# Two expert layers: rows taken and put by tables over the slots, in place of scatters and gathers over the tokens

## Chip, core and metric

One core of a Trainium2 chip runs the whole kernel. The metric is the device time of one execution in microseconds (us), the median of several. Engines: TensorE (PE in the profile; PEld is its weight load), VectorE (DVE), ScalarE (ACT), GpSimd (POOL) and the queue of SyncE (SPq). All DMAs of the core are moved by the same 16 DMA engines.

## What is computed

Twelve residual sublayers, each followed by a layer norm, over x of 2 x 1024 tokens by 256 features. The change touches two of them, both mixtures of 8 experts with a hidden size of 1024:

```python
def _L1_ffn_ref(x, wr, br, w1, b1, w2, b2):        # each token goes to one expert
    expert_id = argmax(x @ wr + br)
    y[e] = gelu(x @ w1[e] + b1[e]) @ w2[e] + b2[e]
    return y[expert_id]
def _L2_ffn_ref(x, Wr, W1, W2):                    # each token has two, of 640 places each
    probs = softmax(x @ Wr); topk_probs, topk_experts = top_k(probs, 2)
    for e in range(8):
        g, idx = top_k(gates of the tokens that chose e, 640)
        y = y.at[idx].add(g * (relu(x[idx] @ W1[e]) @ W2[e]))
    return y
```

## The kernel before

`x_tok` (128 x 16 x 256, f32) holds x by token in SBUF: tile n has tokens 128n to 128n + 127. Each expert layer has two stages with a barrier between them, a router stage and an experts stage.

**Router stages** (`top1_router_stage`, from L1717; `top2_router_stage`, from L1821). VectorE works through a chain of small steps, each waiting for the one before (`step`), with a few products by TensorE between. The result is `core.slots`: for each token, and for each of its choices, the row (slot) that it has in a buffer sorted by expert, plus `slot_gates`. In the first layer also `group_rows`, the expert whose weights each group of slots needs. SP loads the next stage's early data (`following.load`, L1745) meanwhile.

**Experts stages** (`sparse_experts_stage`, L1476). A group is a run of slots of one expert. The first layer (`choices == 1`, `dynamic`) has 15 groups: 7 times a pair of 128-slot tiles and then a single tile, and a last pair. The second (`choices == 2`) has 8 groups of 5 tiles. Every group needs one load of weights of 2180 KB, in one of two buffers `w`.

1. POOL sends each of the 16 tiles of `x_tok` (twice in the second layer) by an indirect DMA to its slots in the DRAM buffer `slot_tokens` (`core.xg`), L1674. In the first layer it first issues the weights of groups 0 and 1 (`weights`, L1666).
2. When all have landed (semaphore `scattered`), SP loads the slots of groups 0 and 1 (L1529). In the second layer SP also issues the weights (L1534).
3. For each group, TensorE transposes its tiles (`turn`, L1560; VectorE copies them out, L1623), multiplies by w1 (`up`, L1573; ScalarE's activation, L1610) and by w2 (`down`, L1585; VectorE adds b2, L1632). The order is up(g), turn(g+1), down(g). When group g is done, SP stores it to `slot_outputs` (`core.yg`, L1543), and then come the weights (POOL in the first layer, L1666, SP in the second) and the slots (SP) of group g+2.
4. When the last store has landed, POOL gathers the outputs of each token tile by `slots` into `got`, a ring of 8 (L1687), VectorE adds each to `x_tok` with its gate (`mix`, L1644 and L1648), and the tail does the layer norm: statistics by VectorE (L2718, L2722), roots by POOL (L2728, L2730, put among the gathers by `ROOTS`), norm by VectorE (L2738), transposes by TensorE (L2749), copies by ScalarE (L2756).

`clear_slots` (L128) zeroes 5120 KB and 4096 KB of the two DRAM buffers during an early attention stage.

Of the kernel before, what the change touches and what calls it, by code (L numbers as in the profile page):

```python
# [24 lines left out]
P = 128  # L25
B, T, D = 2, 1024, 256
N = B * T
# [51 lines left out]
class Core:  # L79


    def __init__(self, nc, A):
# [508 lines left out]
def head_mixing_stage(nc, core, early, room):  # L591
# [10 lines left out]
    with Mem(nc, "L0_attn") as m:  # L602
# [38 lines left out]
        def _(sp):  # L641
# [14 lines left out]
            sp.dma_start(core.spare[:], A["spare"]).then_inc(core.loaded, 16)  # L656
            sp.wait_ge(core.loaded, 32)
# [203 lines left out]
def masked_heads_stage(nc, core, early, bit):  # L861
# [11 lines left out]
    with Mem(nc, name) as m:  # L873
# [27 lines left out]
        @block.sync  # L901
        def _(sp):
            bit.load(sp)
            clear_slots(core, sp)
# [571 lines left out]
def sparse_experts_stage(nc, core, name, func, choices, order, dynamic, keys):  # L1476
# [19 lines left out]
    RING = 8  # L1496
    with Mem(nc, name) as m:
# [9 lines left out]
        got = m.sb("got", [P, RING, choices, D])  # L1507
# [7 lines left out]
        ROOTS = {11: (0,), 15: (1, 2, 3)}  # L1515
        sem = {n: m.sem(n) for n in ("scattered", "xg_turned", "xg_copied", "h_mm", "act_done", "y_mm", "y_copied", "mixed", "first_mixed")}
        gathered = [m.sem(f"gathered{r}") for r in range(RING)]
# [4 lines left out]
        def rows(dram, g):  # L1522
            _, lo, t = order[g]
            return dram[lo:lo + t * P, :].rearrange("(s p) d -> p s d", p=P)
# [1907 lines left out]
```

## Time and profile before

| | us |
|---|---|
| median of 3 runs | 2992.47 (2991.74 to 2993.08) |
| the profiled execution, its own time | 2988.46 |
| its span (first to last instruction) | 2986.5 |
| TensorE busy | 2409.2 (81% of the span) |
| VectorE busy | 1509.9 (51%) |
| ScalarE busy | 829.6 (28%) |
| GpSimd busy | 445.6 (15%) |

The span is cut here into stages by the time of their first instructions. The first layer's router runs from 1071 to 1083.6 us, its experts stage runs to 1342 us; the second layer's router runs from about 1938 to 1990 us, its experts stage to 2394 us. A view of stretches gives the busy time of each engine in each of them; a view in order of time gives single instructions with the idle time of their engine before them and what ended it. DMAs are shown where they are issued, and a line of its own gives the time from issue to landing.

### The profile page before, as it was taken

What the parts mean: (1) busy time and instruction counts of PE and PEld (TensorE: products, weight loads), DVE (VectorE), ACT (ScalarE), POOL (GpSimd) and SP (SyncE); (2) the same over time, 40 slices, a digit from 0 to 9 for tenths busy, and PEclk for the clock granted to TensorE, in tenths of its full rate; (3) what the DMA queues carried; (4) which work ended last, traced back from release to release, by engine and by line L of the source; (5) the groups of instructions that cost most, each with busy time, mean ns of one, the idle gap of its engine ahead of it and who ended that gap; (6) DMA issues with size and microseconds to landing.
All of it is one profiled execution on the core that took longest, in us unless ns stands there. A gap on an engine that the chain in (4) does not pass through costs nothing. (4 is left out here: it accounts for less than half of the span.)

```text
span 2986.5 us, 35097 instructions
## 1 busy us (share of the span) xinstructions
PE 2409.2 (81%) x13955; PEld 1667.2 (56%) x13955; DVE 1509.9 (51%) x2580; ACT 829.6 (28%) x1163; POOL 445.6 (15%) x319
## 2 busy tenths in 40 slices
PE   6776866738888859957999998826999389999888
PEld 4565743412223747744667666724777267777764
DVE  7996866458774420034554564550111445545543
ACT  1111656313556112223332431101111022212122
POOL 3332320220000120020000001021000420000010
PEclk8988878877999969978999999658999699999979
DMA  3003000062430024523222320022221210000000
GB/s 104 0 1 142 29 29 1 22 131 43 67 62 23 11 105 180 213 101 108 80 71 60 90 70 21 20 104 84 100 96 57 65 51 17 17 11 17 1 30 29
DMA packets 80192, 183.87 MB, mean 62 GB/s; under 512 B 15870, under 2 KB 46591, under 8 KB 76464
## 3 DMA queue, kind: packets, MB, share of 16 engines
q1 hardware_dynamic: 73280, 135.80, 16.0%
q0 software_dynamic: 6768, 46.07, 4.2%
q8 instruction: 100, 1.64, 0.2%
q14 instruction: 44, 0.36, 0.0%
HBM read 148.87 MB, written 32.77 MB: 61 GB/s over the span
## 5 line engine op out<-in xcount | busy, mean ns | idle before, releaser
L1573 PE MATMUL L_ffn_h_ps<-L_ffn_xgT,L_ffn_w 128*128 128x512 f32 (+2 forms) x992 | 233.0, 391 | 11.9 <-DMA L_ffn_w<-in_L_ffn_w,group_rows 9.4
L2144 PE MATMUL L_attn_X<-xT,L_attn_w 128*128 128x512 f32 x512 | 227.2, 596 | 0.0
L1585 PE MATMUL L_ffn_y_ps<-L_ffn_w,L_ffn_h 128*128 128x256 f32 x1008 | 223.0, 381 | 4.0 <-ACT L_ffn_h L1610 3.9
L527 DVE TENSOR_REDUCE L_attn_neg<-L_attn_R 128x1 f32<-128x512 f32 (+3 forms) x304 | 187.1, 657 | 53.6 <-PE L_attn_R L404 52.2
L1610 ACT ACTIVATE L_ffn_h<-L_ffn_h_ps,L_ffn_w 128x640 f32<-128x640 f32 (+2 forms) x184 | 101.6, 553 | 401.7 <-PE L_ffn_h_ps L1573 400.0
L1585 PEld LDWEIGHTS L_ffn_y_ps<-L_ffn_w,L_ffn_h 128*128 128x128 f32 x1008 | 189.7, 190 | 32.8 <-ACT L_ffn_h L1610 7.9
L1573 PEld LDWEIGHTS L_ffn_h_ps<-L_ffn_xgT,L_ffn_w 128*128 128x128 f32 x992 | 153.6, 192 | 92.2 <-issue 64.2
L404 PE MATMUL L_attn_R<-L_attn_K,L_attn_Q 104*128 104x512 bf16 (+3 forms) x384 | 118.8, 360 | 83.7 <-DVE L_attn_K L521 48.9
L493 ACT ACTIVATE L_attn_probs<-L_attn_S 128x1024 f32<-128x1024 f32 (+1 forms) x192 | 147.2, 812 | 78.3 <-PE L_attn_S L450 77.6
L1623 DVE COPY L_ffn_xgT<-L_ffn_t_ps 128x256 f32<-128x256 f32 x63 | 24.6, 421 | 279.4 <-PE L_ffn_t_ps L1560 279.4
L2144 PEld LDWEIGHTS L_attn_X<-xT,L_attn_w 128*128 128x128 f32 x512 | 94.9, 190 | 110.3 <-issue 108.5
L1632 DVE TENSOR_TENSOR L_ffn_yg<-L_ffn_y_ps,L_ffn_w 128x256 f32<-128x256 f32 x63 | 26.8, 425 | 224.7 <-PE L_ffn_y_ps L1585 224.7
L2440 PE MATMUL L_attn_X<-xT,L_attn_w 128*128 128x512 f32 x256 | 118.2, 606 | 7.0 <-DMA L_attn_w<-in_L_attn_w 6.4
L404 PEld LDWEIGHTS L_attn_R<-L_attn_K,L_attn_Q 104*128 104x128 bf16 x384 | 33.4, 99 | 157.4 <-DVE L_attn_neg L527 95.3
L1687 POOL DMA_INDIRECT L_ffn_got<-slot_outputs,slots x48 | 46.0, 958 | 348.4 <-DMA slot_outputs<-L_ffn_yg 334.6
L450 PE MATMUL L_attn_S<-L_attn_Q,L_attn_K 107*128 107x512 bf16 (+3 forms) x384 | 95.3, 333 | 2.0 <-ACT L_attn_probs L493 1.9
L845 POOL TENSOR_TENSOR L_attn_v_all<-L_attn_q,L_attn_kv 128x2048 f32<-128x2048 f32 x16 | 73.8, 4615 | 141.1 <-DVE L_attn_q L778 125.2
L2665 POOL TENSOR_TENSOR L_attn_prod<-L_attn_k_sum,L_attn_qs 128x1024 f32<-128x1024 f32 x16 | 37.7, 2358 | 350.0 <-DVE L_attn_qs L2637 350.0
L2224 ACT ACTIVATE L_attn_bc<-L_attn_bc 128x1024 f32<-128x1024 f32 x32 | 33.8, 1057 | 191.1 <-DVE L_attn_bc L2297 191.1
L2343 POOL TENSOR_TENSOR L_attn_sq_sum<-L_attn_sq_sum,L_attn_sq 128x1024 f32<-128x1024 f32 x14 | 33.0, 2359 | 347.1 <-ACT L_attn_sq L2234 347.1
L437 PE MATMUL L_attn_O<-L_attn_probs,L_attn_v_all 128*32 128x512 f32 (+3 forms) x768 | 81.5, 502 | 0.1
L2440 PEld LDWEIGHTS L_attn_X<-xT,L_attn_w 128*128 128x128 f32 x256 | 48.5, 195 | 56.5 <-issue 55.1
(503 smaller groups left out, 4754.2 us busy)
## 6 DMA issues: line engine op xcount, KB each, us to landing
L_ffn_w<-in_L_ffn_w SPq DMA_DIRECT2D x8, 2180.0 KB, 9.3
L_attn_bc<-decays SPq DMA_DIRECT2D x32, 512.0 KB, 6.4
L_attn_w<-in_L_attn_w SPq DMA_DIRECT2D x16, 640.0 KB, 3.9
L_attn_bp<-decays SPq DMA_DIRECT2D x32, 256.0 KB, 7.1
L_attn_Q<-L_attn_q_parts SPq DMA_DIRECT2D x48, 128.0 KB, 5.0
L_attn_K<-L_attn_k_parts SPq DMA_DIRECT2D x48, 128.0 KB, 7.7
L_attn_w<-in_L_attn_w SPq DMA_DIRECT2D x16, 384.0 KB, 3.0
slot_tokens<-zero SPq DMA_DIRECT2D x1, 5120.0 KB, 24.6
```

The costliest lines, as they stand in the source:

```text
L404: mm = nc.tensor.matmul(R[n % 2][:, u * wdt:(u + 1) * wdt], Q[0:KM, par, j0 + u, tt * P:(tt + 1) * P], K[0:KM, par, j0 + u, c * CW:c * CW ...
L437: mm = nc.tensor.matmul(O[32 * j:32 * j + 32, lo:CW], v_all[:, it, gt, 32 * j:32 * j + 32], probs[:, (2 * n + j // 2) % 4, j % 2, lo:CW], ...
L450: mm = nc.tensor.matmul(S[e % 2][:, j % 2, lo:CW], K[0:KS, par, j, gt * P:(gt + 1) * P], Q[0:KS, par, j, tc * CW + lo:(tc + 1) * CW], star ...
L493: nc.scalar.activation(probs[:, e % 4, :, lo:CW], S[e % 2][:, :, lo:CW], ACT.Exp, scale=SCALE).then_inc(exp_done, 1)
L527: nc.vector.tensor_reduce(neg[:, c, j0:j0 + heads, tt], R[n % 2][:, 0:heads * width(tt, c)].rearrange("p (h k) -> p h k", h=heads), X_AXIS ...
L845: nc.gpsimd.tensor_tensor(prod[n % 2][:, h, :, :], q[n % 2][:, h, :].unsqueeze(2).broadcast_to([P, HALF, H, DH]), keys(n).unsqueeze(1).bro ...
L1573: ins = nc.tensor.matmul(h_ps[f % 2][:, lo // CW, 0:hi - lo], w1[u][:, kt, f * P:(f + 1) * P], xgT[u][:, kt, lo:hi], start=kt == 0, stop=k ...
L1585: ins = nc.tensor.matmul(y_ps[k % 2][:], h[:, f, t * P:(t + 1) * P], w2[u][:, f, :], start=f == 0, stop=f == FT - 1)
L1610: nc.scalar.activation(h[:, f, 0:n], h_ps[f % 2][:].rearrange("p c n -> p (c n)")[:, 0:n], func, bias=b1[g % 2][:, f:f + 1]).then_inc(sem[ ...
L1687: nc.gpsimd.indirect_dma_start(got[:, n % RING, c, :], None, outputs, at).then_inc(gathered[n % RING], 16)
L2144: ins = nc.tensor.matmul(x[:, c * CW:(c + 1) * CW], w[1 - par][:, kt, r, :], xT[:, kt, b * T + c * CW:b * T + (c + 1) * CW], start=kt == 0 ...
L2440: ins = nc.tensor.matmul(x[:, c * CW:(c + 1) * CW], w[o][:, kt, r, :], xT[:, kt, b * T + c * CW:b * T + (c + 1) * CW], start=kt == 0, stop ...
```

## The change

A table over the slots takes the place of the one over the tokens. The router stages turn `slots` into `takes` (the token of each slot) and `puts` (the row of the output buffer for each slot): a class `SlotTokens` compares every token's slot with a row of numbers (`at_row`, 0/1 in bf16) and with the slot's tile (`at_column`), TensorE multiplies the two (one product for each of the 16 or 32 token tiles), and seven steps make the tables. K is 16 in the first layer and 32 in the second, G (tiles of slots) 23 and 40. SP stores `x_tok` to the DRAM buffer `token_rows` at the start of each router stage.

In the experts stages POOL takes a group's rows from `token_rows` straight into `xg` (one indirect DMA for each tile of slots), and puts each output tile, as soon as it is copied, into `token_outputs` by token. All of it is in one order on POOL, with the weights of the first layer. At the end SP (and ScalarE's queue for the second choice) fetches the outputs of two token tiles at a time with plain DMAs into `got`, which now holds all tiles. `clear_outputs` zeroes 4096 KB. The routers load three more small constants early. The diff, cut to its core:

```diff
-        SLOTS, SPARE = N * 2 * 5 // 4, 2 * N
-        self.xg = nc.dram_tensor("slot_tokens", (SLOTS + SPARE, D), F32, kind="Internal").ap()
-        self.yg = nc.dram_tensor("slot_outputs", (SLOTS + SPARE, D), F32, kind="Internal").ap()
-        self.slots = sb("slots", [P, 2, N // P], mybir.dt.uint32)
+        SLOTS = N * 2 * 5 // 4
+        self.x_rows = nc.dram_tensor("token_rows", (N, D), F32, kind="Internal").ap()
+        self.outputs = nc.dram_tensor("token_outputs", (3 * N + SLOTS, D), F32, kind="Internal").ap()
+        self.takes = sb("takes", [P, SLOTS // P], mybir.dt.uint32)
+        self.puts = sb("puts", [P, SLOTS // P], mybir.dt.uint32)
-        self.spare = sb("spare", [P, 2, N // P], F32)
-        self.zeroed_rows = self.xg[0:SLOTS, :], self.yg[SLOTS:SLOTS + SPARE, :]
-        self.zeroed = nc.alloc_semaphore("slots_zeroed")
+        self.zeroed = nc.alloc_semaphore("outputs_zeroed")
+        self.x_stored = nc.alloc_semaphore("token_rows_stored")
...
-def clear_slots(core, sp):
-    for dram in core.zeroed_rows:
-        to = dram.rearrange("(s p) d -> p s d", p=P)
-        sp.dma_start(to, over(core.zero[:], to.shape[1])).then_inc(core.zeroed, 16)
+def clear_outputs(core, sp):
+    to = core.outputs[0:2 * N, :].rearrange("(s p) d -> p s d", p=P)
+    sp.dma_start(to, over(core.zero[:], to.shape[1])).then_inc(core.zeroed, 16)
+def store_tokens(core, sp):
+    sp.dma_start(core.x_rows.rearrange("(n p) d -> p n d", p=P), core.x_tok[:]).then_inc(core.x_stored, 16)
...
-    RING = 8
+    UNITS = NT // 2
...
-        got = m.sb("got", [P, RING, choices, D])
+        got = m.sb("got", [P, choices, NT, D])
...
+        same_parity = lambda g: sum(size[g % 2:g + 1:2])
+        def fetch(eng, u, c):
+            lo = first_row + c * N + 2 * u * P
+            eng.dma_start(got[:, c, 2 * u:2 * u + 2, :], core.outputs[lo:lo + 2 * P, :].rearrange("(n p) d -> p n d", p=P)).then_inc(gathered[u], 16)
+        def all_put(eng):
+            for g in (groups - 2, groups - 1):
+                eng.wait_ge(y_stored[g % 2], 16 * same_parity(g))
         @block.sync
         def _(sp):
-            def load(g):
-                sp.dma_start(xg[g % 2][:, 0:size[g], :], rows(core.xg, g)).then_inc(xg_loaded[g % 2], 16)
             def weights(g):
                 if not dynamic:
                     n = order[g][0]
             for u in range(2):
                 weights(u)
-            sp.wait_ge(sem["scattered"], 16 * choices * NT)
-            for u in range(2):
-                load(u)
-            for g in range(groups):
-                sp.wait_ge(sem["y_copied"], before[g + 1])
-                sp.dma_start(rows(core.yg, g), yg[g % 2][:, 0:size[g], :]).then_inc(y_stored[g % 2], 16)
-                if g + 2 < groups:
-                    weights(g + 2)
-                    load(g + 2)
+            for g in range(2, groups):
+                sp.wait_ge(sem["y_copied"], before[g - 1])
+                weights(g)
+            all_put(sp)
+            for u in range(UNITS):
+                fetch(sp, u, 0)
...
-                pe.wait_ge(xg_loaded[u], 16 * (g // 2 + 1))
+                pe.wait_ge(xg_loaded[u], 16 * same_parity(g))
...
+            if choices == 2:
+                all_put(act)
+                for u in range(UNITS):
+                    fetch(act, u, 1)
+            for u in range(UNITS):
                 tail.copy(act, u)
...
-                dve.wait_ge(gathered[r], 16 * choices * (n // RING + 1))
...
+            for u in range(UNITS):
+                dve.wait_ge(gathered[u], 16 * choices)
...
-            if dynamic:
-                weights(0)
-                weights(1)
-            for n in range(NT):
-                for c in range(choices):
-                    at = bass.IndirectOffsetOnAxis(core.slots[:, c, n:n + 1], 0)
-                    nc.gpsimd.indirect_dma_start(core.xg, at, core.x_tok[:, n, :], None).then_inc(sem["scattered"], 16)
-            if dynamic:
-                for g in range(2, groups):
-                    pool.wait_ge(sem["y_copied"], before[g - 1])
+            def take(g):
+                for t in range(size[g]):
+                    at = bass.IndirectOffsetOnAxis(core.takes[:, order[g][1] // P + t:order[g][1] // P + t + 1], 0)
+                    nc.gpsimd.indirect_dma_start(xg[g % 2][:, t, :], None, core.x_rows, at).then_inc(xg_loaded[g % 2], 16)
+            def put(g, t):
+                pool.wait_ge(sem["y_copied"], before[g] + t + 1)
+                at = bass.IndirectOffsetOnAxis(core.puts[:, order[g][1] // P + t:order[g][1] // P + t + 1], 0)
+                nc.gpsimd.indirect_dma_start(core.outputs, at, yg[g % 2][:, t, :], None).then_inc(y_stored[g % 2], 16)
+            pool.wait_ge(core.x_stored, 16 * choices)
+            for g in range(2):
+                if dynamic:
                     weights(g)
-            for u in range(2):
-                pool.wait_ge(y_stored[u], 16 * ((groups + 1 - u) // 2))
-            outputs = core.yg[0:before[groups] * P, :] if choices == 1 else core.yg
-            for n in range(NT):
-                if n >= RING:
-                    pool.wait_ge(sem["mixed"], n - RING + 1)
-                for c in range(choices):
-                    at = bass.IndirectOffsetOnAxis(core.slots[:, c, n:n + 1], 0)
-                    nc.gpsimd.indirect_dma_start(got[:, n % RING, c, :], None, outputs, at).then_inc(gathered[n % RING], 16)
-                for b in ROOTS.get(n, ()):
-                    tail.root(pool, b)
+                take(g)
+            for g in range(groups):
+                if g + 2 < groups:
+                    pool.wait_ge(sem["xg_turned"], before[g + 1])
+                    take(g + 2)
+                for t in range(size[g]):
+                    put(g, t)
+                if dynamic and g + 2 < groups:
+                    weights(g + 2)
+            for b in range(len(tail.batches)):
+                tail.root(pool, b)
...
+    items = {"column": tile(P), "tile_no": tile(choices * NT), "unused": tile(groups), "wr": tile(KT, E_), "first": tile(E_), "same8": tile(P), "earlier8": tile(P)}
...
+    def vector(self, dve, step, slot):
+        V, w, K, G = self.nc.vector, self.w, self.K, self.G
+        step(V.tensor_scalar(self.slots[:], slot, -1.0, None, ALU.add))
+        step(V.tensor_scalar(self.part_i[:, 0, :], self.slots[:], 7, None, ALU.logical_shift_right))
+        step(V.tensor_scalar(self.part_i[:, 1, :], self.slots[:], P - 1, None, ALU.bitwise_and))
+        step(V.tensor_copy(self.parts[:], self.part_i[:]))
+        step(V.tensor_tensor(self.at_column[:], over(w["column"][:, 0:G], K), along(self.parts[:, 0, :], G), ALU.is_equal))
+        V.tensor_tensor(self.named[:, :, 0, :], self.at_column[:], along(w["tile_no"], G), ALU.mult).then_inc(self.named_set, 1)
+        V.tensor_scalar(self.named[:, :, 1, :], self.at_column[:], self.core.part[:], None, ALU.mult).then_inc(self.named_set, 1)
+        for c in range(K // 8):
+            of = slice(8 * c, 8 * c + 8)
+            V.tensor_tensor(self.at_row[:, of, :], over(w["column"], 8), along(self.parts[:, 1, of], P), ALU.is_equal).then_inc(self.rows_set, 1)
+    def tensor(self, pe, ps):
+        pe.wait_ge(self.named_set, 2)
+        for k in range(self.K):
+            if k % 8 == 0:
+                pe.wait_ge(self.rows_set, k // 8 + 1)
+            mm = self.nc.tensor.matmul(ps[:, 0:2 * self.G], self.at_row[:, k, :], self.named[:, k, :, :].rearrange("p a g -> p (a g)"),
+                                       start=k == 0, stop=k == self.K - 1)
+        mm.then_inc(self.tokens_mm, 1)
+    def tables(self, dve, step, ps):
+        V, core, G = self.nc.vector, self.core, self.G
+        dve.wait_ge(self.tokens_mm, 1)
+        step(V.tensor_copy(self.where[:], ps[:, G:2 * G]))
+        step(V.scalar_tensor_tensor(self.blank[:], ps[:, 0:G], 0.0, self.w["unused"], ALU.is_equal, ALU.mult))
+        step(V.tensor_scalar(self.again[:], ps[:, 0:G], NT + 0.5, float(N), ALU.is_ge, ALU.mult))
+        step(V.scalar_tensor_tensor(self.where[:], ps[:, 0:G], float(P), self.where[:], ALU.mult, ALU.add))
+        step(V.scalar_tensor_tensor(core.puts[:, 0:G], self.where[:], float(self.first_row - P), self.blank[:], ALU.add, ALU.add))
+        step(V.scalar_tensor_tensor(self.where[:], self.where[:], -float(P), self.again[:], ALU.add, ALU.subtract))
+        step(V.tensor_scalar(core.takes[:, 0:G], self.where[:], 0.0, None, ALU.max))
...
+            store_tokens(core, sp)
             following.load(sp)
-            sp.wait_ge(core.zeroed, 32)
...
-            step(V.tensor_scalar(core.slots[:, 0, :], mx[:], -1.0, None, ALU.add))
+            tokens.vector(dve, step, mx[:])
             step(V.memset(core.slot_gates[:, 0, :], 1.0))
+            tokens.tables(dve, step, i_ps)
...
-            step(V.scalar_tensor_tensor(spare_at[:], slot[:], 0.0, core.spare[:], ALU.is_equal, ALU.mult))
-            step(V.tensor_tensor(slot[:], slot[:], spare_at[:], ALU.add))
-            step(V.tensor_scalar(core.slots[:], slot[:], -1.0, None, ALU.add))
+            tokens.vector(dve, step, slot[:].rearrange("p c n -> p (c n)"))
             step(V.tensor_tensor(tmp[:], numbers, along(slot[:, 0, :], E_), ALU.is_equal))
             step(V.tensor_tensor(hot1[:], gates, tmp[:], ALU.mult))
             step(V.tensor_reduce(core.slot_gates[:, 0, :], hot1[:], X_AXIS, ALU.add))
             step(V.tensor_tensor(hot2[:], gates, hot1[:], ALU.subtract))
             step(V.tensor_reduce(core.slot_gates[:, 1, :], hot2[:], X_AXIS, ALU.add))
+            tokens.tables(dve, step, g_ps)
```

## Rows read from the trace of the kernel before

**Rows 1.** Stretches: length, then PE, PEld, DVE, ACT, POOL busy, granted clock, DMA share.
```profile
1115.80:1308.50 192.70, 178.42 (x890) 147.83 (x890) 18.02 (x44) 52.08 (x121) 12.27 (x13) 0.99 0.48 179
...
1990.90:2041.90 51.00, 10.05 (x46) 8.01 (x47) 5.83 (x10) 1.93 (x6) 31.21 (x32) 0.57 0.53 196
2041.90:2336.90 295.00, 290.23 (x1222) 206.72 (x1222) 30.55 (x75) 50.82 (x64) 0.00 (x0) 0.99 0.21 75
```

**Rows 2.** In order of time, start of the first experts stage: start, duration, instruction.
```profile
1087.02 1.21 POOL L1666 DMA_INDIRECT L_ffn_w<-in_L_ffn_w,group_rows  x1 [28.82 <-issue]
...
1114.05 1.11 PE L1560 MATMUL L_ffn_t_ps<-ident,L_ffn_xg 128*128 128x128 f32 x4 [22.26 <-DMA L_ffn_xg<-slot_tokens]
...
1115.78 3.75 PE L1573 MATMUL L_ffn_h_ps<-L_ffn_xgT,L_ffn_w 128*128 128x256 f32 x8 [0.61 <-DVE L_ffn_xgT L1623]
```

**Rows 3.** In order of time, start of the second experts stage.
```profile
1991.65 1.14 POOL L1674 DMA_INDIRECT slot_tokens<-x_tok,slots  x1 [69.43 <-POOLq L56]
...
2038.10 1.11 PE L1560 MATMUL L_ffn_t_ps<-ident,L_ffn_xg 128*128 128x128 f32 x4 [39.98 <-DMA L_ffn_xg<-slot_tokens]
...
2041.91 19.19 PE L1573 MATMUL L_ffn_h_ps<-L_ffn_xgT,L_ffn_w 128*128 128x512 f32 x64 [0.61 <-DVE L_ffn_xgT L1623]
```

**Rows 4.** Who waited for whom, in both experts stages: total, times, longest.
```profile
PE L_ffn_h_ps L1573 <- DMA L_ffn_w<-in_L_ffn_w,group_rows: 9.4, 7, 1.8
...
DVE x_tok L1644 <- DMA L_ffn_got<-slot_outputs,slots: 9.4, 8, 5.1
...
DVE x_tok L1644 <- DMA L_ffn_got<-slot_outputs,slots: 22.5, 14, 7.9
```

**Rows 5.** Single VectorE instructions of 308, 1024, 1232 and 32 elements.
```profile
1035.82 0.48 DVE L3163 TENSOR_TENSOR L_xattn_s<-L_xattn_s,L_xattn_mx 128x308 f32<-128x308 f32 x1
...
1367.24 1.23 DVE L2295 TENSOR_TENSOR L_attn_bc<-L_attn_bc,L_attn_ct 128x1024 f32<-128x1024 f32 x1 [7.89 <-DMA L_attn_bp<-decays]
...
1991.82 0.80 DVE L2907 TENSOR_SCALAR L_xattn_fill<-L_xattn_fill 128x1232 f32<-128x1232 f32 x1
...
L1948 DVE SCALAR_TENSOR_TENSOR L_router_spare_at<-L_router_slot,spare x1: 193/193/193, 1987.7 to 1987.7; 128x32 f32<-128x32 f32 x1
```

**Rows 6.** The page: bf16 weight loads of TensorE; DMA issues with their landing.
```profile
L404 PEld LDWEIGHTS L_attn_R<-L_attn_K,L_attn_Q 104*128 104x128 bf16 x384 | 33.4, 99 | 157.4 <-DVE L_attn_neg L527 95.3
...
slot_tokens<-zero SPq DMA_DIRECT2D x1, 5120.0 KB, 24.6
...
L_ffn_xg<-slot_tokens SPq DMA_DIRECT2D x8, 256.0 KB, 2.9
...
slot_tokens<-x_tok,slots POOLq DMA_INDIRECT x48, 2.5
```

**Rows 7.** Issue to landing: weights at 1087.0, 1158.9, 1167.7; scatters at 1995.6 and 1996.9.
```profile
DMA to landing us min/median/max: 9.2/9.2/9.2
...
DMA to landing us min/median/max: 9.7/9.7/9.7
...
DMA to landing us min/median/max: 8.4/8.4/8.4
...
DMA to landing us min/median/max: 9.0/9.5/9.9
```

**Rows 8.** In order of time, norms on VectorE beside an indirect issue of POOL.
```profile
2374.39 2.64 DVE L2738 TENSOR_SCALAR x_tok<-x_tok,L_ffn_tail_mv,L_ffn_tail_rstd 128x256 f32<-128x256 f32 x8
...
2375.61 0.95 POOL L1687 DMA_INDIRECT L_ffn_got<-slot_outputs,slots  x1 [0.30 <-issue]
```

**Rows 9.** In order of time, last output of each experts stage and its first mix.
```profile
1308.04 0.42 DVE L1632 TENSOR_TENSOR L_ffn_yg<-L_ffn_y_ps,L_ffn_w 128x256 f32<-128x256 f32 x1 [2.93 <-PE L_ffn_y_ps L1585]
...
1313.62 0.48 DVE L1644 SCALAR_TENSOR_TENSOR x_tok<-L_ffn_got,slot_gates,x_tok 128x256 f32<-128x256 f32 x1 [5.15 <-DMA L_ffn_got<-slot_outputs,slots]
...
2336.46 0.42 DVE L1632 TENSOR_TENSOR L_ffn_yg<-L_ffn_y_ps,L_ffn_w 128x256 f32<-128x256 f32 x1 [3.03 <-PE L_ffn_y_ps L1585]
...
2344.80 0.48 DVE L1644 SCALAR_TENSOR_TENSOR x_tok<-L_ffn_got,slot_gates,x_tok 128x256 f32<-128x256 f32 x1 [7.92 <-DMA L_ffn_got<-slot_outputs,slots]
```

More of the change, by code:

```diff
@@ L1611, in _ @@
                                          bias=b1[g % 2][:, f:f + 1]).then_inc(sem["act_done"], 1)
-            for u in range(NT // 2):
+            if choices == 2:
[3 more added lines that the diff above has]
+            for u in range(UNITS):
                 tail.copy(act, u)
@@ L1627, in biased @@
                 if g >= 2:
-                    dve.wait_ge(y_stored[g % 2], 16 * (g // 2))
+                    dve.wait_ge(y_stored[g % 2], 16 * same_parity(g - 2))
                 for t in range(size[g]):
@@ L1647, in mix @@
                     dve.wait_ge(sem["first_mixed"], n + 1)
-                    ins = nc.vector.scalar_tensor_tensor(x, got[:, r, 1, :], core.slot_gates[:, 1, n:n + 1], x, ALU.mult, ALU.add)
+                    ins = nc.vector.scalar_tensor_tensor(x, got[:, 1, n, :], core.slot_gates[:, 1, n:n + 1], x, ALU.mult, ALU.add)
                 ins.then_inc(sem["mixed"], 1)
-            for u in range(NT // 2):
+            for u in range(UNITS):
+                dve.wait_ge(gathered[u], 16 * choices)
                 for n in tail.tiles(u):
@@ L1708, in router_early @@
     tile = lambda *s: ([P, *s], F32)
-    items = {"wr": tile(KT, E_), "first": tile(E_), "same8": tile(P), "earlier8": tile(P)}
+    choices, groups = (1, 2 * PAIRS + SINGLES) if name == "L1_router" else (2, E_ * CAP // P)
+    items = {"column": tile(P), "tile_no": tile(choices * NT), "unused": tile(groups), "wr": tile(KT, E_), "first": tile(E_), "same8": tile(P), "earlier8": tile(P)}
     if name == "L1_router":
@@ L1714, in router_early, with __init__ @@
     return Early(nc, name, A, items, ctx=ctx)
+class SlotTokens:
+    def __init__(self, m, core, w, name, choices, groups, first_row):
+        self.nc, self.core, self.w, self.name, self.G, self.K, self.first_row = core.nc, core, w, name, groups, choices * NT, first_row
+        K, G = self.K, groups
+        self.slots, self.part_i = m.sb("slots", [P, K], I32), m.sb("slot_parts_i", [P, 2, K], I32)
+        self.parts = m.sb("slot_parts", [P, 2, K])
+        self.at_row = m.sb("at_row", [P, K, P], BF16)
+        self.at_column = m.sb("at_column", [P, K, G])
+        self.named = m.sb("named", [P, K, 2, G], BF16)
+        self.where, self.again, self.blank = m.sb("where", [P, G]), m.sb("again", [P, G]), m.sb("blank", [P, G])
+        self.named_set, self.rows_set, self.tokens_mm = m.sem("named_set"), m.sem("rows_set"), m.sem("tokens_mm")
+    def vector(self, dve, step, slot):
[28 more added lines that the diff above has]
+        step(V.tensor_scalar(core.takes[:, 0:G], self.where[:], 0.0, None, ALU.max))
@@ L1962, in top1_experts_stage @@
     order = [x for j in range(SINGLES) for x in (pair(j), single(j))] + [pair(PAIRS - 1)]
-    sparse_experts_stage(nc, core, "L1_ffn", ACT.Gelu, 1, order, True, keys)
+    sparse_experts_stage(nc, core, "L1_ffn", ACT.Gelu, 1, order, True, keys, 2 * N)
 def top2_experts_stage(nc, core, keys, router):
     top2_router_stage(nc, core, keys.early, router)
-    sparse_experts_stage(nc, core, "L2_ffn", ACT.Relu, 2, [(e, CAP * e, CAP // P) for e in range(E_)], False, keys)
+    sparse_experts_stage(nc, core, "L2_ffn", ACT.Relu, 2, [(e, CAP * e, CAP // P) for e in range(E_)], False, keys, 0)
 HL = 16
@@ L3396, in more_arrays @@
     a["part"] = p_[:, None].astype(f)
-    a["spare"] = (N * 2 * 5 // 4 + 1 + p_[:, None] + np.arange(2 * NT) * P).astype(f).reshape(P, 2, NT)
+    for l, groups, free, choices in (("L1_router_", 2 * PAIRS + SINGLES, N, 1), ("L2_router_", E_ * CAP // P, 3 * N, 2)):
+        a[l + "column"] = bc(p_.astype(f))
+        a[l + "tile_no"] = bc(1 + np.arange(choices * NT).astype(f))
+        a[l + "unused"] = (free + P + p_[:, None] + P * np.arange(groups)).astype(f)
     a["same64"] = (p_[:, None] // DL == p_ // DL).astype(f)
```

29 lines of the change are left out of this document (14 added, 15 removed).

## The prediction

> **What bounds the kernel now.** I read the view of stretches first. In both experts stages TensorE works 178.4 of 192.7 us and 290.2 of 295.0 us while the groups run, at a granted clock of 0.99, and only 10 of the 51 us ahead of the second stage's first group [rows 1]. So the middle of each stage belongs to TensorE, and the change can win at the two ends of each stage, and lose in the middle (if it delays a load) or in the routers. The view in order of time shows the starts: TensorE waits 22.3 us and 40.0 us for `xg`, which waits for 16 and 32 scatters [rows 2, 3]. At the ends, VectorE waits for gathers for 9.4 and 22.5 us [rows 4]. All of this is on the path that sets the end, since a barrier closes each stage.
>
> **Router of the first layer: +7.6 us.** Every added VectorE step follows the last, so all of it is exposed. Small steps cost 0.19 us for 32 elements [rows 5], with the wait for each other about 0.23. Slot, tile, row and copy are four, one of which replaces the old conversion: +0.7. `at_column` and the first `named` have 16 x 23 = 368 elements. From 0.48 us for 308 and 1.23 for 1024 [rows 5] I interpolate 0.54 each; the second `named` is one with a constant, and of those 1232 elements took 0.80 us [rows 5], so 0.4: together 1.5. `at_row` is two comparisons of 1024 elements, 1.23 each: 2.5. TensorE's last 8 products wait for the second. A bf16 weight load took 0.099 us [rows 6]; at a low clock and with the semaphores I take 1.3 for the eight (0.8 to 4). The seven steps of the tables: 1.6. Sum 7.6, from 5.5 (wide comparisons at half price) to 10.5.
>
> **Router of the second layer: +10.7 us.** Small steps +0.7, less 0.5 for two steps on spare rows that go. 32 x 40 = 1280 elements: 1.5 twice and 0.8. Four wide comparisons: 5.0. The five steps on gates of 128 elements stand between and cover the last products. Tables 1.7. Sum 10.7 when nothing is rounded (8 to 14.5).
>
> **Store of the rows, zeroes, constants: 0.** 2048 KB go out at the router's start. The zeroing of 5120 KB landed after 24.6 us [rows 6], so by size this takes about 10, from 1071 on, and is done before POOL's wait, which comes after 1087.0 + 7.6 in the first layer. The next stage's early data queue behind it on SP and have the longer router as cover. If that failed it would cost a few us, which the router's bound holds. The zeroing and its halving lie beside an attention stage in which nobody waits for it; six small loads are early.
>
> **Start of the first experts stage: -16.7 us.** POOL now issues weights(0), two takes, weights(1), one take, in place of 16 scatters. The first load landed 9.2 us after its issue [rows 7], at 1096.2. The takes are issued 1.5 and 2.8 us after it and queue behind it in the same queue; I add 1.1 us for them. TensorE's transposes to its first product took 1.73 us (1114.05 to 1115.78) [rows 2]: 1087.0 + 9.2 + 1.1 + 1.7 = 1099.0, against 1115.8 [rows 2]. Bounds -15 and -17.5 (takes land with the weights).
>
> **Start of the second: -32.0 us.** The five takes of group 0 go out from 1991.65 at 1.26 us each, beside the two loads of weights on SP. The scatters now stand exactly there. The fourth and fifth, issued at 1995.6 and 1996.9, needed 9.0 to 9.9 us to land [rows 7], against a median of 2.5 [rows 6]: the weights' packets are in the way on the same 16 engines. So the fifth take lands at about 1996.9 + 9.2 = 2006.1. The transposes to the first product took 3.8 us (2038.10 to 2041.91) [rows 3]: 2009.9 instead of 2041.9. Bounds: -29, if the takes come only after all of both loads and a read is slower than a write; -37.5, if they land after 2.5 to 4 us.
>
> A rule of the Trainium skill speaks against takes and puts beside VectorE. In this trace the norms by VectorE run from 2374.39 to 2377.03 while POOL issues a gather at 2375.61 in 0.95 us, the usual time [rows 8]. "SBUF — State Buffer", section "Who interferes with whom", says that a `tensor_scalar` with both sides in SBUF can take the port pair that GpSimd writes descriptors through, and that the other then fully blocks. By that rule the first takes of the second stage, beside two such instructions of 0.80 us, would be issued up to 1.6 us late and the sum would be 44.1 instead of 45.7; by the row it is 45.7, and I go by the row.
>
> **Middle of the first stage: +5 us.** This is what the change puts at risk. POOL issues weights(g+2) only after the last put of group g, 1.26 us later than now. Behind a single tile there is no slack: TensorE waits for weights 7 times, 9.4 us in total [rows 4], so the slip is paid seven times. Against it stands lighter traffic. The loads that are waited for landed after 9.7 us with a store and a load of 256 KB beside them, others after 8.4 with half of that [rows 7]; with those two gone I take 0.7 us off, and add 0.2 for the put's packets ahead. 7 x (1.26 - 0.7 + 0.2) = 5. Bounds: 7 x -0.3 = -2, if the landing falls by 1.6, and +11, if it doesn't fall. The other weights have a pair's 15 us as cover. A group costs POOL at most 5 takes and 5 puts, 12.6 us, under the second stage's 37 us (295/8), so there it adds nothing. Takes are one group ahead; a late one would be paid by TensorE at `turn`, behind `up`. Puts block only POOL. y_stored is waited for two groups later.
>
> **Ends: -3.7 and -16.6 us.** Now: last output at 1308.46 and 2336.88, first mix 5.2 and 7.9 us later [rows 9]. After: 0.3 us to POOL, a put that lands after 2.5 us, a fetch of 256 KB that lands after 2.9 [rows 6], 0.2 between: 5.9. So +0.7 and -2.0. Then VectorE no longer waits for the other gathers, which were paced by POOL at 1.26 us each: 9.4 - 5.1 = 4.3 and 22.5 - 7.9 = 14.6 us [rows 4] go. VectorE's own work is next: two tiles need over 1.8 us of it, a fetch of 256 KB a good microsecond of transfer. Bounds -2.5 to -4.5 and -14 to -18.
>
> **Sum.** +7.6 - 16.7 + 5 - 3.7 = -7.8 for the first layer and +10.7 - 32.0 - 16.6 = -37.9 for the second: -45.7. The profiled execution took 2988.46 us in all, 4.0 below the median of the runs; from it 2942.8, and from the median of 2992.5 the forecast: 2946.8, rounded to 2947.
>
> **Rivals.**
> - *Takes overtake the weights.* The fifth take lands about 2.5 us after its issue, the second layer starts 6.6 us earlier: -52, 2940. For it: they are on another queue. Against: the scatters' 9.0 to 9.9 us [rows 7].
> - *Weights pay in full.* No relief from the lighter traffic, +11 instead of +5, and the products and takes at their high bounds (+5): -35, 2958. For it: seven waits without slack [rows 4], an extra issue ahead of each load.
> - *POOL's one queue becomes the bound, slower.* If each indirect DMA had to land before the next moves, a pair and a single tile of the first stage (25 us now, 1115.8 to 1308.5 less the last pair's 17, by 7) would take 2 loads of 9.2 and 6 takes and puts of 2.6: 34. That is +63 in place of +5: +12, 3005. It decides from 7.2 us more for each such period. Against it: scatters were issued every 1.27 us, landed after 2.5, and were not slowed.
> - *It doesn't bring the starts forward.* The takes hang on something that I missed (the stored rows, the tables), and about 49 us of gain at the starts don't come; the rest is +3, 2995.
>
> **How the numbers follow.** Forecast 0.62, takes first 0.13, weights in full 0.19, slower 0.04, no start 0.02. The range goes from 2936 (the first rival with a cheap router) to 2962 (the second with late takes), leaving about 0.15 out. A measurement of this kernel tells 0.2%, 6 us, from nothing: faster 0.94, same 0.02, slower 0.04.
>
> **What would show it.** The first `up` product comes about 18 us after POOL's first take in the second layer and 12 us after the first weights in the first; the first layer's seven waits for weights total about 14 us (9.4 now); VectorE has no waits for DMAs in the tails but the first; the steps from the slots to the end of the routers are 7.6 and 10.7 us longer. I am wrong if TensorE waits for takes between groups, if `at_row` is far from 1.23 us, or if the early data of the next stage wait behind the store.

## The result and the profile after

The changed kernel takes 2964.4 us (median of four runs, 2962.7 to 2966.2) against 2992.1 for the kernel before: 0.991 of it, with a 95% interval of 0.989 to 0.992. It is 27.7 us faster where 45.7 were forecast, and lies 2.4 us above the upper end of the range. The direction was as forecast, the ends came within 0.2 us, and the two starts gained 1.9 and 3.5 us less than forecast. The term that failed is the middle of the first experts stage, which lost 21 us in place of 5.

Both profiled executions, cut at the same instructions (predicted; measured in us):

| Part | predicted | measured |
|---|---|---|
| router 1, from its scores to POOL's first issue | +7.6 | +6.4 (17.5 to 23.9) |
| start 1, from there to the first product | -16.7 | -14.8 (28.8 to 13.9) |
| **middle 1, first product to last output** | **+5** | **+21.2** (192.7 to 213.9) |
| end 1, to the next stage's first load | -3.7 | -3.7 (33.7 to 30.0) |
| router 2, from the slots to POOL's first take | +10.7 | +10.1 (4.8 to 14.9) |
| start 2 | -32.0 | -28.5 (50.3 to 21.8) |
| middle 2 | 0 | +0.7 (295.0 to 295.6) |
| end 2 | -16.6 | -16.4 (57.3 to 40.8) |
| stretches that the change does not touch | 0 | +2.9 (-3.6, +4.1, +2.4) |
| sum | -45.7 | -22.1 (spans 2986.5 to 2964.4) |

The gain here (22.1) is smaller than that of the medians (27.7) because of the two executions that were profiled: the one before took 2988.5 us, 3.6 under its median, the one after 2966.2, 1.8 above.

The stretches of the kernel after (length, then PE, PEld, DVE, ACT, POOL busy, granted clock, DMA share, GB/s). They answer to [rows 1]:
```profile
1087.80:1103.80 16.00, 7.95 (x33) 6.32 (x33) 1.44 (x3) 1.37 (x4) 5.37 (x6) 0.71 0.76 270
1103.80:1317.00 213.20, 191.49 (x890) 158.38 (x890) 17.61 (x43) 52.01 (x121) 53.11 (x55) 0.92 0.44 165
...
2010.00:2030.00 20.00, 7.87 (x39) 7.04 (x40) 3.80 (x5) 1.93 (x6) 10.08 (x10) 0.67 0.87 289
2030.00:2329.00 299.00, 293.17 (x1231) 208.86 (x1229) 32.59 (x80) 50.78 (x64) 66.69 (x69) 0.99 0.23 76
```
The second line holds the whole surprise. TensorE executes the same 890 instructions as before, but is busy with them for 191.5 us in place of 178.4, at a granted clock of 0.92 in place of 0.99. A wait adds idle time, not busy time, so 13 of the 21 us are not waiting.

TensorE in order of time, the changed kernel, first experts stage (start, duration, instruction, idle before and what ended it):
```profile
1102.06 1.11 PE L1562 MATMUL L_ffn_t_ps<-ident,L_ffn_xg 128*128 128x128 f32 x4 [7.43 <-DMA L_ffn_xg<-token_rows,takes]
1103.79 3.75 PE L1575 MATMUL L_ffn_h_ps<-L_ffn_xgT,L_ffn_w 128*128 128x256 f32 x8 [0.62 <-DVE L_ffn_xgT L1629]
...
1133.95 10.22 PE L1575 MATMUL L_ffn_h_ps<-L_ffn_xgT,L_ffn_w 128*128 128x256 f32 x32 [3.41 <-DMA L_ffn_w<-in_L_ffn_w,group_rows]
...
1163.45 8.86 PE L1575 MATMUL L_ffn_h_ps<-L_ffn_xgT,L_ffn_w 128*128 128x256 f32 x32 [2.89 <-DMA L_ffn_w<-in_L_ffn_w,group_rows]
...
1190.83 8.86 PE L1575 MATMUL L_ffn_h_ps<-L_ffn_xgT,L_ffn_w 128*128 128x256 f32 x32 [2.12 <-DMA L_ffn_w<-in_L_ffn_w,group_rows]
```
The same group in the kernel before:
```profile
1168.71 7.22 PE L1573 MATMUL L_ffn_h_ps<-L_ffn_xgT,L_ffn_w 128*128 128x256 f32 x32 [1.83 <-DMA L_ffn_w<-in_L_ffn_w,group_rows]
```
The up-products of all seven pairs that wait for weights took 7.22 us before. After, they took 10.2 us once, 8.9 four times and 8.8 twice. In finer stretches of the changed kernel (same columns), the granted clock is whole while TensorE waits and falls as the products begin:
```profile
1160.50:1163.40 2.90, 0.06 (x1) 0.00 (x0) 0.42 (x1) 0.00 (x0) 1.70 (x2) 1.00 0.57 235
1163.40:1166.80 3.40, 3.35 (x9) 2.77 (x10) 0.00 (x0) 0.54 (x2) 2.15 (x3) 0.59 0.78 233
1166.80:1170.20 3.40, 3.40 (x15) 2.79 (x15) 0.00 (x0) 1.80 (x4) 0.00 (x0) 0.91 0.98 415
```
A mean of 0.59 is a mixture of the two levels, 2.4 and 1.2 GHz, with most of the stretch at the lower.

Why the wait grew is in POOL's rows of the changed kernel:
```profile
1180.79 0.99 POOL L1681 DMA_INDIRECT token_outputs<-L_ffn_yg,puts  x1 [2.36 <-DVE L_ffn_yg L1638]
1182.08 0.98 POOL L1671 DMA_INDIRECT L_ffn_w<-in_L_ffn_w,group_rows  x1 [0.31 <-issue]
```
and in the kernel before:
```profile
1158.94 0.94 POOL L1666 DMA_INDIRECT L_ffn_w<-in_L_ffn_w,group_rows  x1 [15.24 <-DVE L_ffn_yg L1632]
```
In the changed kernel the put stands between VectorE's last output and the load. Over the seven loads the issue comes 1.58 us after that output, where it came 0.27 before. Issue to landing went from 9.27 to 9.10 us on average (load's start on POOL to the products' start on TensorE). So 7 x (1.31 - 0.17) = 8 us of waiting, and the view of waits agrees, 9.4 [rows 4] to 17.3:
```profile
PE L_ffn_h_ps L1575 <- DMA L_ffn_w<-in_L_ffn_w,group_rows: 17.3, 7, 3.4
```

### The profile page after: what moved, and what is told of

Read it like the earlier page. It is cut to its first block and busy times, and to the rows that moved or that the text cites. A ratio compares the mean times of both kernels' runs of the same rounds, so it can differ in the third digit from the quotient of the medians.

```text
span 2964.4 us, 35239 instructions
## 1 busy us (share of the span) xinstructions
PE 2428.4 (82%) x13995; PEld 1683.9 (57%) x14003; DVE 1522.2 (51%) x2610; ACT 829.0 (28%) x1163; POOL 476.3 (16%) x349
## 3 DMA queue, kind: packets, MB, share of 16 engines
q8 instruction: 100, 1.64, 0.2%
## 5 line engine op out<-in xcount | busy, mean ns | idle before, releaser
L1575 PE MATMUL L_ffn_h_ps<-L_ffn_xgT,L_ffn_w 128*128 128x512 f32 (+2 forms) x992 | 247.0, 409 | 19.8 <-DMA L_ffn_w<-in_L_ffn_w,group_rows 17.3
L1575 PEld LDWEIGHTS L_ffn_h_ps<-L_ffn_xgT,L_ffn_w 128*128 128x128 f32 x992 | 164.6, 203 | 103.1 <-issue 65.5
L1681 POOL DMA_INDIRECT token_outputs<-L_ffn_yg,puts x63 | 61.8, 980 | 372.0 <-DVE L_ffn_yg L1638 372.0
L2291 ACT ACTIVATE L_attn_bc<-L_attn_bc 128x1024 f32<-128x1024 f32 x32 | 33.8, 1057 | 194.1 <-DVE L_attn_bc L2364 194.1
```

What stands on the lines that cost most here:

```text
L1575: ins = nc.tensor.matmul(h_ps[f % 2][:, lo // CW, 0:hi - lo], w1[u][:, kt, f * P:(f + 1) * P], xgT[u][:, kt, lo:hi], start=kt == 0, stop=k ...
L1681: nc.gpsimd.indirect_dma_start(core.outputs, at, yg[g % 2][:, t, :], None).then_inc(y_stored[g % 2], 16)
```

## Experiments

**One theory and its rivals.** A: the longer wait lets TensorE's clock fall, so each wait is paid a second time in the products behind it. B: the products are slower because takes and puts move beside them. The first profile repeated, the weights ahead of the put, nine useless products and the held load ran on one chip; the second repeat, four useless products, the ladder and both edits together on another; the last four on a third; each beside the kernel before. "Middle" below is from the first up-product to the end of the last product in the profiled execution: 192.2 before, 213.4 after (the table above goes on to the last output, 0.5 us later). "Waits" are the seven waits for weights in it. A pair is called slow when its 32 up-products take 8.6 us or more in place of 7.2.

### The changed kernel again

> The changed kernel once more, so that the runs beside it have a partner on the same chip. Both theories: within 2 us of 2964.4 (28 us under the kernel before), the first stage's seven waits for weights 17 us in all, the 32 up-products behind each of them 8.8 us where the kernel before took 7.2. If a stretch that the change does not touch differs by several us between two profiles of this same kernel, the leftover of 2 to 4 us per stretch in the first comparison is the spread of single executions and not an effect of the change.

> The changed kernel a third time, as partner of the other runs of this chip: 2956 to 2966 us by the spread of the first two. Both theories: the waits for weights are within 0.3 us of the earlier ones for each load, since they come from issue and landing; the up-products behind them take 8.8 us in most groups but not in all, as one of the seven took 7.2 behind a wait of 2.65 us in the second profile.

Measured: 2957.7 us (2955.6 to 2963.2) and 2963.6 us (2958.7 to 2963.9), ratios 0.989 [0.987, 0.991] and 0.990 [0.988, 0.992]. The middles are 209.9 and 209.8, the waits 17.5 us both times, and in each one pair of seven kept its 7.22 us, behind waits of 2.65 and 2.25. So the forecast's upper end, 2962, is inside the spread of this kernel. Untouched stretches differ by more than I had thought: from the next stage's first product to the second router's slots the profiles of this study show 637 to 649 us for the same instructions, and POOL's first issue comes anywhere from 1088.1 to 1098.9 in kernels that are equal up to there. The leftover of +2.9 us in the first table is no larger than this spread.

### The weights ahead of the last put

```
 # POOL, groups of the first layer
-for t in range(size[g]):
+for t in range(size[g] - 1):
     put(g, t)
 if dynamic and g + 2 < groups:
+    pool.wait_ge(sem["y_copied"], before[g + 1])
     weights(g + 2)
+put(g, size[g] - 1)
```

> The changed kernel, but in the first experts stage POOL issues weights(g+2) ahead of the last put of group g, so 1.26 us earlier; the put and its traffic are all still there. Theory A (the longer wait lets TensorE's clock fall, and the products behind it pay again): the seven waits go back from 17.3 to about 8.5 us, the up-products behind them from 8.8 to 7.2 us, the stage loses 9 + 13 = 22 us: 2943. Theory B (the products are slower because takes and puts move beside them, whatever TensorE did before): the waits go back by 9 us, the products stay at 8.8: 2956.

Measured: 2944.8 us (2938.3 to 2958.0), ratio 0.985 [0.982, 0.987], 13 us under the changed kernel beside it. Its wait for weights (total, times, longest), its TensorE in order of time and its middle as a stretch:
```profile
PE L_ffn_h_ps L1575 <- DMA L_ffn_w<-in_L_ffn_w,group_rows: 8.7, 7, 2.1
```
```profile
1136.10 7.22 PE L1575 MATMUL L_ffn_h_ps<-L_ffn_xgT,L_ffn_w 128*128 128x256 f32 x32 [1.43 <-DMA L_ffn_w<-in_L_ffn_w,group_rows]
1161.79 7.22 PE L1575 MATMUL L_ffn_h_ps<-L_ffn_xgT,L_ffn_w 128*128 128x256 f32 x32 [2.06 <-DMA L_ffn_w<-in_L_ffn_w,group_rows]
```
```profile
1108.60:1300.00 191.40, 178.28 (x890) 147.77 (x890) 17.59 (x43) 52.03 (x121) 53.02 (x55) 0.99 0.50 186
```
All seven pairs are back at 7.22 us and the clock at 0.99, with every take and put still there. The middle is 191.5, 18.5 us under the changed kernel beside it and no longer than before the change. B falls as it was put: with the takes and puts beside them, the products are as fast as before. The medians show 13 of these 18.5 us; the kernel's five times spread over 20 us, so this is no contradiction.

### Work of no use in the wait

```
 # TensorE, up(g), constants FILL = 9 or 4
+pe.wait_ge(sem["xg_copied"], before[g + 1])
+if dynamic and g >= 2 and size[g] == 2:
+    for n in range(FILL):
+        nc.tensor.matmul(h_ps[0][:, 0, 0:2 * P], core.ident[:],
+                         xgT[u][:, n % KT, 0:2 * P], start=True, stop=True)
 pe.wait_ge(w_loaded[u], 16 * (g // 2 + 1))
-pe.wait_ge(sem["xg_copied"], before[g + 1])
```

> The changed kernel, but in each pair's group TensorE does nine products of 128x128 by 128x256 of no use (about 2 us at the high clock) ahead of its wait for the weights. The loads and their landings are unchanged. Theory A: the first real product of a pair starts within 0.3 us of where it started, but at the high clock: 7.2 us for the 32 products in place of 8.8, the granted clock of the stage back from 0.92 to about 0.99, 13 us less: about 2952. Theory B: the products stay at 8.8 us, and the time at 2964.

> The changed kernel with four products of no use (eight instructions, 1.8 us) ahead of each pair's wait for weights, in place of nine (eighteen instructions, 4.05 us), which covered the whole wait of 2.0 to 2.8 us and more. Theory A: what is left of each wait is 0.2 to 1.5 us, all up-products take 7.2 us, the stage's middle falls from 210 to about 200 us, and the time by about 10 us against the changed kernel beside it: 2948. Theory B (products are slow because of the traffic, and nine fillers only seemed to help): they stay at 8.8, and the time does not move.

Measured with nine: 2961.6 us (2958.9 to 2963.5). TensorE in order of time:
```profile
1163.71 4.05 PE L1571 MATMUL L_ffn_h_ps<-L_ffn_xgT,ident 128*128 128x256 f32 x18
1167.60 7.12 PE L1579 MATMUL L_ffn_h_ps<-L_ffn_xgT,L_ffn_w 128*128 128x256 f32 x32
```
I had mis-sized the filler. A product in f32 is two instructions, so nine cost 4.05 us and covered the whole wait and more. But it is the cleanest of the runs: issue and traffic are those of the changed kernel, TensorE has no idle gap, and all seven pairs take 7.12 us. What the clock gave back, the excess of filler took: the middle is 210.6. So the idle gap is a necessary part of the cause of the slow products.

Measured with four: 2961.4 us (2956.2 to 2969.1), against 2963.6 for its partner, which is no difference that these runs can tell. In the profile the middle fell from 209.8 to 205.7. Six pairs with 0.6 to 1.6 us left of the wait took 7.22; the seventh did not:
```profile
1165.27 1.89 PE L1571 MATMUL L_ffn_h_ps<-L_ffn_xgT,ident 128*128 128x256 f32 x8
1169.58 8.86 PE L1579 MATMUL L_ffn_h_ps<-L_ffn_xgT,L_ffn_w 128*128 128x256 f32 x32 [2.42 <-DMA L_ffn_w<-in_L_ffn_w,group_rows]
```
Of the expected 10 us 4 came. Of the 6 that are missing, 3.9 are loads that landed after 9.66 us on average in place of 9.11 (this one after 10.8), and 1.6 the pair that stayed slow. Why the loads landed later stays open.

### The slip alone, in the kernel before

```
 # POOL, kernel before; DELAY per group
 pool.wait_ge(sem["y_copied"], before[g - 1])
+if DELAY.get(g):
+    nc.gpsimd.memset(idle[:, 0:DELAY[g]], 0.0).then_inc(idled, 1)
+    pool.wait_ge(idled, ...)
 weights(g)
```

> The kernel before, with nothing of the change in it, but POOL sets a scratch tile of 256, 128, 1024, 768 and 2048 elements per partition ahead of the loads of groups 6, 8, 10, 12 and 14 (about 0.5, 0.4, 1.1, 0.9 and 2.0 us). TensorE's waits for weights should be 1.3 and 1.8 us (groups 2 and 4, untouched), then about 1.5, 1.9, 2.1, 2.4 and 3.3. Theory A: the products behind the first three or four stay at 7.2 us and those behind waits of over 2 us take about 8.8; the kernel is slower by the added waits, 4.9 us, and by some 5 us of clock: +10. Theory B: without takes and puts all stay at 7.2 us, +5.

Measured: 2999.9 us, ratio 1.003 [1.001, 1.005]; middle 197.5, +5.3 (one of its pairs also waited 2.0 us for its rows). The waits were 1.35, 2.04, 1.22, 1.31, 1.69, 2.46 and 3.08 us, and all seven pairs took 7.22. That refutes A in its simple form: a wait of 3.08 us need not bring the clock down. I formed C (the takes and puts are needed as well) and D (a long wait is needed, but where it falls counts too).

> The kernel before, where POOL sets 1024 elements of a scratch tile (0.95 us, and 0.3 to the issue) ahead of each of the seven loads that TensorE waits for: the slip of the changed kernel without its takes and puts. The waits should go from 9.4 to 18 us in all, each 2.2 to 3.1. In the ladder, waits of 2.46 and 3.08 us were followed by products of 7.2, so three theories now stand. A (a wait of over 2 us brings the clock down by itself): behind five or more of the seven a pair takes 1.6 us longer, and the middle goes from 192 to about 211 us, +19. C (it needs the takes and puts beside it): none does, +9. D (a long wait is needed, but where it falls also counts): one to four do, +10 to +15.

> As before_late, with 2048 elements (1.80 us and 0.3): the waits 3.1 to 4.0 us, 24 us in all. A and D: the longer the wait the surer the fall, five to seven of seven, the middle at 192 + 15 + 10 = 217 us. C: no fall, 207.

Measured: 3004.4 us, ratio 1.005 [1.003, 1.007], middle 201.0; and 3013.6 us, ratio 1.007 [1.004, 1.009], middle 212.3. Two pairs of seven slowed in the first, five of seven in the second. Four of its seven rows, of both kinds:
```profile
1144.46 10.15 PE L1575 MATMUL L_ffn_h_ps<-L_ffn_xgT,L_ffn_w 128*128 128x256 f32 x32 [3.15 <-DMA L_ffn_w<-in_L_ffn_w,group_rows]
...
1229.80 7.22 PE L1575 MATMUL L_ffn_h_ps<-L_ffn_xgT,L_ffn_w 128*128 128x256 f32 x32 [2.62 <-DMA L_ffn_w<-in_L_ffn_w,group_rows]
...
1255.96 8.86 PE L1575 MATMUL L_ffn_h_ps<-L_ffn_xgT,L_ffn_w 128*128 128x256 f32 x32 [2.39 <-DMA L_ffn_w<-in_L_ffn_w,group_rows]
...
1312.26 7.22 PE L1575 MATMUL L_ffn_h_ps<-L_ffn_xgT,L_ffn_w 128*128 128x256 f32 x32 [3.13 <-DMA L_ffn_w<-in_L_ffn_w,group_rows]
```
This kernel has no take and no put in its middle, so C falls: delay alone brings the clock down, to the same 8.9 or 10.2 us. The waits (14.4 and 20.1 us) were about 4 us shorter than expected, for two reasons: the issue slipped by 1.02 and 1.87 us in place of 1.25 and 2.1, and the loads landed 0.3 us sooner (9.0 and 8.9 on average in place of 9.27).

### The slip with the put behind, and more slip

```
 # as in "the weights ahead of the last put" / as in the changed kernel
+nc.gpsimd.memset(idle[:, 0:1024], 0.0).then_inc(idled, 1)
+pool.wait_ge(idled, g // 2 + 1)
 weights(g + 2)
```

> The changed kernel with the weights' issue ahead of the last put, as in weights_first, but a scratch tile of 1024 elements is set ahead of it: the slip is back (1.25 us) while the put comes after the load. The waits go from 8.7 back to 17.5 us. A: five or more of the seven pairs take 1.6 us longer again, and the middle is 210 as in the changed kernel. C, if it is the put ahead of the load that matters: no fall, middle 200. D: one to four falls, 202 to 207.

> The changed kernel with the same scratch tile between the last put and the weights: waits of 3.3 to 4.7 us, 26 us in all. A and D: all or nearly all pairs take 1.6 us longer or more, as now: the middle is 210 + 9 = 219 us, and the time 9 us above the changed kernel, near 2971. C: the same, as put and wait are both there. If the fall became rarer instead, position would weigh more than length.

Measured: 2957.7 us (2950.6 to 2961.4), middle 203.8, waits 16.1, three pairs slow; and 2975.6 us (2966.6 to 2982.3), middle 221.2, waits 23.8, all seven slow, three of them at 9.7 to 10.1 us. With the put behind the load, the slip brings back 12.3 of the 18.5 us of middle that the order had won (203.8 against 191.5): 7.4 in the waits and 4.9 in three slow pairs. So most of the put's harm is its 1.3 us of issue ahead of the load. That six or seven pairs were slow with the put ahead, and three here, it does not explain.

All profiles of the study but the one with nine useless products, which has no such wait, by the wait ahead of a pair:

| wait for weights | pairs | slow |
|---|---|---|
| under 2 us, any kernel | 33 | 0 |
| 2 us and over, changed kernel and those with the put ahead of the load | 36 | 33 |
| 2 us and over, kernels without it | 22 | 10 |

So D stands as far as these runs go. A wait of 2 us or more is what makes a slow pair possible. The wait's length alone does not settle it: 2.46 and 3.08 us passed, 2.00 did not. Nor does it explain the difference between the two kinds of kernel: among waits of 2.0 to 2.5 us, 18 of 20 were followed by a slow pair with the put ahead and 5 of 12 without. What stays open is why the kernels with the put ahead are hit nearly every time; that the put or its traffic adds to the chance is not ruled out. Their groups follow each other at nearly equal distances (27.4 us three times between the starts of the second to the fifth waiting pair), so each gap may fall where the last one fell; that is argued and was not tested. "TensorE: Matmul & The Clock Gate" in the Trainium skill, section "What's actually happening", says that the gate's measuring does not start with the kernel but runs freely. The spread of one kernel (six of seven slow twice, seven of seven once) is in line with that; no run here tests it. Its section "Why this matters for your kernels" warns of idle gaps that are longer than most of those that did it here (32 of the 43 were of 2.0 to 3.0 us); here the table above decides.

### The first takes ahead of the second load

```
 # SP, start of the second experts stage
-for u in range(2):
-    weights(u)
+weights(0)
+if not dynamic:
+    sp.wait_ge(xg_loaded[0], 16 * size[0])
+weights(1)
```

> The changed kernel, but in the second experts stage SP holds the weights of group 1 until the five takes of group 0 have landed. Theory A (the takes land late because both loads of 2180 KB are ahead of them or beside them on the same 16 engines): the fifth take lands some 7 us after its issue in place of 12.7, the stage starts about 6 us earlier: 2958.5. Theory B (the takes are slow by themselves, or behind the first load alone): the start does not move by more than 1.5 us: 2963 to 2966.

Measured: 2954.5 us (2950.8 to 2964.2), ratio 0.987 [0.985, 0.989], 3.3 us under its partner. The start in the changed kernel, in order of time:
```profile
2011.38 1.15 POOL L1676 DMA_INDIRECT L_ffn_xg<-token_rows,takes  x1 [79.19 <-POOLq L56]
...
2016.60 1.36 POOL L1676 DMA_INDIRECT L_ffn_xg<-token_rows,takes  x1 [0.30 <-issue]
...
2029.35 1.12 PE L1562 MATMUL L_ffn_t_ps<-ident,L_ffn_xg 128*128 128x128 f32 x4 [11.41 <-DMA L_ffn_xg<-token_rows,takes]
```
and with the second load held:
```profile
2021.35 1.35 POOL L1678 DMA_INDIRECT L_ffn_xg<-token_rows,takes  x1 [0.30 <-issue]
...
2028.68 1.12 PE L1564 MATMUL L_ffn_t_ps<-ident,L_ffn_xg 128*128 128x128 f32 x4 [6.00 <-DMA L_ffn_xg<-token_rows,takes]
```
The transposes start 12.7 us after the fifth take's issue; with the load held, 7.3 us. From POOL's first take to the first product it is 16.4 us in place of 21.4 (the second profile of the changed kernel), the 5 to 6 us that A expected. "DMA: Bandwidth & Descriptors" in the Trainium skill, section "Issuing engines are not separate DMA queues", says that transfers of all issuing engines share the same 16 DMA engines; these takes on POOL's queue, late behind loads on SP's, agree.

### Both edits together

> The changed kernel with both edits: the weights' issue ahead of the last put in the first experts stage, and the weights of group 1 held until the takes of group 0 have landed in the second. They touch different stages, so both theories add them up: -13 to -18 us and -4 to -5 us against the changed kernel beside it: about 2938, 1.7% under the kernel before.

Measured: 2938.3 us (2936.5 to 2948.1), ratio 0.982 [0.980, 0.985], 25 us under the changed kernel beside it and 53 under the kernel before. The middle is 194.1 with no slow pair, the start of the second stage 15.9 us. Its longest wait for weights passed without a slow pair:
```profile
1156.27 7.22 PE L1577 MATMUL L_ffn_h_ps<-L_ffn_xgT,L_ffn_w 128*128 128x256 f32 x32 [2.60 <-DMA L_ffn_w<-in_L_ffn_w,group_rows]
```

## Why the prediction was right and wrong

**The step that failed is "Middle of the first stage: +5 us".** It named the right place, the seven loads that slip behind a put, and its "slip" of 1.26 us was 1.31. Two things in it were wrong.
- *The relief.* I took 0.7 us off each load's landing, and added 0.2 for the put, because one waited-for load had landed after 9.7 and one with less beside it after 8.4 [rows 7]. But 9.7 was the slowest of the seven that are waited for; their mean was 9.27, and it became 9.10. A relief of 0.17 in place of a net 0.5, seven times, is 2.3 us; with the slip of 1.31 the term is +8, not +5.
- *What follows a wait.* "The slip is paid seven times" took TensorE to run as before once the weights are there. It pays again: 12.7 us in the products behind the seven waits (3.00 + 4 x 1.64 + 1.62 + 1.54), and 0.6 in the first pair. 7.95 + 12.7 + 0.6 = 21.2. So of the 16 us between forecast and measured, 3 were the loads and 13 the products. The runs show the idle gap to be the cause: fill it, or shorten the waits, and the second payment goes; add it to the kernel before, and it comes. I had the granted clock of 0.57 ahead of the second stage in [rows 1] in view, and priced a low clock only for eight products of the router. With +21 in its place, the forecast's own sum is -29.5, or 2963.

**Routers.** +6.4 and +10.1 for 7.6 and 10.7. In the first, the table's last products held VectorE up for 0.65 us (1084.25 to 1084.90) where 1.3 was written. The two wide comparisons took 2.35 us where 2.5 was written, the four 4.62 for 5.0, and the steps of 1280 elements 1.49 for 1.5:
```profile
1998.20 1.49 DVE L1750 TENSOR_TENSOR L_router_at_column<-L_router_column,L_router_slot_parts 128x1280 f32<-128x1280 f32 x1
...
2001.93 4.62 DVE L1755 TENSOR_TENSOR L_router_at_row<-L_router_column,L_router_slot_parts 128x1024 bf16<-128x1024 f32 x4
```
**Store of the rows.** At nothing, as said: by the page of the changed kernel (KB, us to landing) it lands well ahead of the router's end.
```profile
token_rows<-x_tok SPq DMA_DIRECT2D x2, 2048.0 KB, 8.4
```

**Start of the first stage.** -14.8 for -16.7: the transposes came 12.2 us after POOL's first issue (1089.87 to 1102.06), where 9.2 + 1.1 was written, which is the whole miss; the first product followed after 1.73. Why they came 1.9 us later was not tested. It is just outside its bounds of -15 to -17.5.

**Start of the second.** -28.5 for -32.0, just outside its bound of -29, which stood for exactly what happened: takes that land behind both loads. I took the landing of the scatters that now stand there, 9.0 to 9.9 us [rows 7]; the fifth take needed 12.7.

**Takes beside VectorE.** I went by the row, and the rule that I weighed against it, of "SBUF — State Buffer" in the Trainium skill, section "Who interferes with whom", did not show. POOL's first take of the second stage stood beside two `tensor_scalar` of 0.80 us (2010.73 and 2011.57) and was issued in 1.15 us; the next ones took 0.95. The first scatter before, with 1.14 [rows 3], stood beside the same two, so it is no measure of an undisturbed issue. The first issue of the first stage (a load of weights) is one, with nothing on VectorE beside it: 1.22 us in the changed kernel, 1.21 before [rows 2].

**Ends.** -3.7 and -16.4 for -3.7 and -16.6. VectorE waits for gathered rows once in each stage and never again:
```profile
1323.10 0.88 DVE L1648 SCALAR_TENSOR_TENSOR x_tok<-L_ffn_got,slot_gates,x_tok 128x256 f32<-128x256 f32 x2 [5.40 <-DMA L_ffn_got<-token_outputs]
...
2335.17 0.48 DVE L1648 SCALAR_TENSOR_TENSOR x_tok<-L_ffn_got,slot_gates,x_tok 128x256 f32<-128x256 f32 x1 [6.36 <-DMA L_ffn_got<-token_outputs]
```

**The rivals.** "Takes overtake the weights" is refuted by the 12.7 us. "Weights pay in full" was nearest, and its 2958 is what the second chip measured, but that is luck: its +11 took the relief to be nothing, and the rest of the loss was in the clock. "POOL's one queue becomes the bound" is refuted by a middle of 191.5 us with all takes and puts in place. "It doesn't bring the starts forward" is refuted by the two starts.

**The range.** What it left out was a second price on the same event. It went to +11 for the middle because I bounded the landing and not the engine that waits.

## What to carry to other kernels

Where the bounding engine has short waits between dense stretches, price a longer wait twice: once for the wait, and once for TensorE's products behind it, which here took 1.6 to 3 us more behind most waits of 2 us and over and nothing more behind shorter ones. When an issue is put on a queue that also feeds the bounding engine, put the load that is waited for ahead of it: here that order was worth 13 us in the medians, and 18 in the profiled middle, for a line that moves. And a term of the sum that is to be relieved needs the mean over all its occurrences, not the difference of two of them.

## What the hardware showed that I had not expected

- The granted clock can fall behind a gap as short as 2.00 us: in this stage the 32 up-products of a pair then take 8.86 us in place of 7.22, sometimes 10.2. It never fell behind 33 waits under 2 us, and it did not fall behind some of 2.46 to 3.13.
- Products of no use in a gap kept the clock up, but gave nothing when they were as long as the gap and the loss together: 4.05 us of them gained nothing against 2.0 to 3.3 us of wait.
- A load of 2180 KB that is waited for lands after 8.5 to 10.8 us, by executions and by groups, and the same instructions between the two experts stages took 637 to 649 us in different executions. A term of a few us is to be read in its own stage, and not from the totals.
